# One-hot rows of the degree count: one tensor-with-tensor comparison per group of 512 ids in place of four per-column comparisons

## The reference, cut to what matters

```
ones    = jnp.ones((E,))
deg_in  = segment_sum(ones, dst, num_segments=N)
deg_out = segment_sum(ones, src, num_segments=N)
def layer(h, W, b, act):
    fwd = segment_sum(h[src], dst) / max(deg_in, 1)
    bwd = segment_sum(h[dst], src) / max(deg_out, 1)
    return act(concat([h, fwd, bwd]) @ W + b)
h = relu(layernorm(x));  x = x + layer(layer(h, W1, b1, relu), W2, b2, id)
h = relu(layernorm(x));  x = x + mlp(concat([h, segment_sum(edge_attr, dst), u[0]]))
```

## Time and profile before

| what | us |
|---|---|
| median of 3 executions | 4206.28 |
| fastest and slowest of them | 4197.02, 4271.05 |
| the profiled execution | 4203.99 |
| its span in the trace | 4202.4 |
| busy: PE, DVE, ACT, POOL | 3672.5, 3159.2, 2308.9, 3040.7 |
| first stage: first pick to last pick issued | 10.72 to 335.79 |

### The profile page before, as it was taken

The page is one execution under the profiler, slowest core; times in us unless marked ns, Lnnn a source line. Parts: engine busy times, 40 slices in busy tenths (PEclk is TensorE's granted clock), DMA queues, the critical chain, the costliest instruction groups (busy, mean ns, idle before and its releaser), DMA issues.

```text
span 4202.4 us, 94475 instructions
## 1 busy us (share of the span) xinstructions
PE 3672.5 (87%) x25698; PEld 3238.8 (77%) x25698; DVE 3159.2 (75%) x11005; ACT 2308.9 (55%) x5788; POOL 3040.7 (72%) x2962
## 2 busy tenths in 40 slices
PE   8817898888886888888888888699999999999999
PEld 2207888888876787887887787688888888888888
DVE  8816888888886555555565555489999999999998
ACT  0013444444444555555555555477777777777776
POOL 7866888888887677777777777666666666666665
PEclk9958999999998999999999999899999999999999
DMA  7676777777776677777787777777777777777775
GB/s 253 245 256 174 176 179 176 178 184 181 182 174 148 165 185 188 189 191 177 192 194 182 186 193 186 160 154 158 158 160 158 158 159 158 159 159 159 158 160 121
DMA packets 818427, 742.95 MB, mean 177 GB/s; under 512 B 200444, under 2 KB 629896, under 8 KB 818282
## 3 DMA queue, kind: packets, MB, share of 16 engines
q1 hardware_dynamic: 637702, 522.72, 42.0%
q0 software_dynamic: 166208, 167.10, 27.8%
q10 hardware_dynamic: 14372, 51.75, 3.1%
HBM read 355.07 MB, written 334.83 MB: 164 GB/s over the span
## 4 chain that ended last, share of the span: by engine, by line
PE 40%; DMA 7%; DVE 6%; issue 6%; another core or an unknown queue 4%; ACT 3%; SPq 2%; POOL 1%; DVEq 0%; ACTq 0%; POOLq 0%
PE bank L1569 8%; DMA normed<-in_x_dram 6%; PE bank L1583 4%; PE bank L1582 4%; PE bank L1584 4%; PE bank L1547 2%; PE bank L1540 2%; PE bank L1542 2%; PE bank L1546 2%; PE bank L1541 2%; PE bank L1556 2%; DVE stats L1169 2%; PE bank L1477 2%; PE bank L1478 1%
## 5 line engine op out<-in xcount | busy, mean ns | idle before, releaser
L632 POOL DMA_INDIRECT node<-summed,rep_index x392 | 624.7, 1594 | 230.6 <-issue 158.9
L585 POOL DMA_INDIRECT sums<-summed,rep_index x392 | 621.1, 1584 | 149.1 <-issue 122.2
L663 POOL TENSOR_TENSOR resid<-node_out,b3s 128x128 f32<-128x128 f32 x784 | 335.9, 457 | 478.4 <-DVE rows L1291 475.5
L1241 DVE SCALAR_TENSOR_TENSOR z<-bank,bias,small 128x512 f32<-128x512 f32 x784 | 568.0, 744 | 67.0 <-ACT small L897 58.3
L897 ACT ACTIVATE small<-bank,bias_small 128x512 f32<-128x512 f32 x784 | 535.4, 683 | 104.0 <-PE bank L1584 49.3
L673 POOL TENSOR_TENSOR z_lo<-z,z_hi 128x512 fp32r<-128x512 f32 x392 | 495.5, 1283 | 9.4 <-ACT z_hi L928 9.4
L1477 PE MATMUL bank<-hx,W1s 128*128 128x128 f32 x1568 | 325.2, 291 | 179.2 <-ACT hx L837 150.6
L617 POOL DMA_INDIRECT ends<-sums,index x392 | 381.6, 974 | 121.8 <-issue 121.5
L1477 PEld LDWEIGHTS bank<-hx,W1s 128*128 128x128 f32 x1568 | 251.1, 201 | 213.4 <-issue 213.2
L1569 PE MATMUL bank<-w3s,z 128*128 128x128 f32 x3136 | 382.4, 275 | 3.1 <-DVE z L1241 3.1
L1569 PEld LDWEIGHTS bank<-w3s,z 128*128 128x128 f32 x3136 | 365.7, 192 | 4.1 <-DVE z L1241 4.0
(11 more groups left out here) (152 smaller groups left out, 9549.8 us busy)
## 6 DMA issues: line engine op xcount, KB each, us to landing
node<-blank SPq DMA_DIRECT2D x98, 768.0 KB
sums<-zeros ACTq DMA_DIRECT2D x98, 512.0 KB
normed<-in_x_dram SPq DMA_DIRECT2D x196, 256.0 KB
rows<-sums SPq DMA_DIRECT2D x196, 256.0 KB
y<-node_out SPq DMA_DIRECT2D x196, 256.0 KB
node_out<-node SPq DMA_DIRECT2D x196, 256.0 KB, 3.2
node_out<-y POOLq DMA_DIRECT2D x196, 256.0 KB, 4.2
a_parts<-a_pair SPq DMA_DIRECT2D x784, 64.0 KB, 2.6
```

Of the source, the lines that this page charges most:

```text
L585: pool.indirect_dma_start(sums1, bass.IndirectOffsetOnAxis(ap=rep_index[:, b, s:s + 1], axis=0), summed[:, b, s, 0:F], None, compute_op=AL ...
L632: pool.indirect_dma_start(node1, bass.IndirectOffsetOnAxis(ap=rep_index[:, b, s:s + 1], axis=0), summed[:, b, s, :], None, compute_op=ALU. ...
L1241: dve.scalar_tensor_tensor(out=z[:, m, :], in0=bank[first_bank + m][:], scalar=bias[:, m:m + 1], in1=small[:, m, :], op0=ALU.add, op1=ALU. ...
```

## The change

Only the counting is touched. A group's four columns are compared in one instruction with each table: the tables `iota_hi` and `iota_lo` hold every value four times side by side, `hilo` is stored in f16 with the four columns of a group adjacent, and `tensor_tensor` compares the table with the four ids of the group, repeated along the table. The four one-hot rows of a group so lie interleaved: element (value, s) at position 4 * value + s. The buffers are two, each for a whole group. TensorE reads column s of the buffer with a step of four elements (8 bytes), for the stationary and for the moving operand. The counts and the banks are the same. The loop over groups is written out, as before.

```diff
-        iota_hi = sb("iota_hi", [P, HALF], F16)
-        iota_lo = sb("iota_lo", [P, 2 * P], F16)
+        iota_hi = sb("iota_hi", [P, HALF, 4], F16)
+        iota_lo = sb("iota_lo", [P, 2 * P, 4], F16)
...
-        hilo = sb("hilo", [P, 2, 4, G])
-        onehot_hi = sb("onehot_hi", [P, 4, HALF], BF16)
-        onehot_lo = sb("onehot_lo", [P, 4, 2 * P], BF16)
+        hilo = sb("hilo", [P, 2, G, 4], F16)
+        onehot_hi = sb("onehot_hi", [P, 2, HALF, 4], BF16)
+        onehot_lo = sb("onehot_lo", [P, 2, 2 * P, 4], BF16)
...
-            pool.iota(iota_hi[:], pattern=[[1, HALF]], base=0, channel_multiplier=0,
+            pool.iota(iota_hi[:], pattern=[[1, HALF], [0, 4]], base=0, channel_multiplier=0,
...
-            pool.iota(iota_lo[:], pattern=[[1, 2 * P]], base=0, channel_multiplier=0,
+            pool.iota(iota_lo[:], pattern=[[1, 2 * P], [0, 4]], base=0, channel_multiplier=0,
...
-            dve.tensor_copy(hilo[:].rearrange("p a s g -> p a (s g)"), part[:]).then_inc(s_vprep, 1)
+            for a in range(2):
+                last = dve.tensor_copy(hilo[:, a].rearrange("p g s -> p s g"), part[:, a].rearrange("p (s g) -> p s g", g=G))
+            last.then_inc(s_vprep, 1)
...
-            def onehots(st, i):
-                s = st.half + 2 * i
-                if st.after(2):
-
-                    dve.wait_ge(s_count, 2 * st.k + i - 3)
-                dve.tensor_scalar(onehot_lo[:, s, :], iota_lo[:], hilo[:, 1, s, bass.ds(st.g, 1)], None, ALU.is_equal)
-                dve.tensor_scalar(onehot_hi[:, s, :], iota_hi[:], hilo[:, 0, s, bass.ds(st.g, 1)], None, ALU.is_equal)\
+            for g in range(G):
+                b = g % 2
+                if g >= 2:
+
+                    dve.wait_ge(s_count, 4 * (g - 1))
+                dve.tensor_tensor(onehot_lo[:, b], iota_lo[:], hilo[:, 1, g, :].unsqueeze(1).to_broadcast([P, 2 * P, 4]), ALU.is_equal)
+                dve.tensor_tensor(onehot_hi[:, b], iota_hi[:], hilo[:, 0, g, :].unsqueeze(1).to_broadcast([P, HALF, 4]), ALU.is_equal)\
                     .then_inc(s_onehot, 1)
...
-            def count(st):
-                for i in range(2):
-                    s = st.half + 2 * i
-                    pe.wait_ge(s_onehot, 2 * st.k + i + 1)
+            for g in range(G):
+                pe.wait_ge(s_onehot, g + 1)
+                for s in range(4):
                     for h in range(2):
-                        last = pe.matmul(bank[2 * i + h][:, 0:HALF], onehot_lo[:, s, h * P:(h + 1) * P], onehot_hi[:, s, :],
-                                         start=(st.known and st.k == 0), stop=st.last)
+                        last = pe.matmul(bank[2 * (s // 2) + h][:, 0:HALF], onehot_lo[:, g % 2, h * P:(h + 1) * P, s],
+                                         onehot_hi[:, g % 2, :, s], start=(g == 0 and s % 2 == 0), stop=(g == G - 1 and s % 2 == 1))
                     last.then_inc(s_count, 1)
```

More of the change, by code:

```diff
@@ L277, in ticks @@
                 tick(lambda n, t=t: Step(STEPS // 4 - 1, t - n))
-        def written_out(tick):
-            for k in range(STEPS):
-                tick(lambda n, k=k: Step(0, k - n))
         QUADS = G // 4
@@ L981, in rstd_of @@
                 dve.reciprocal(rstd[:, st.b, 0:n], spread[:, st.b, 0:n]).then_inc(s_rstd, 1)
-            def onehots(st, i):
-                s = st.half + 2 * i
-                if st.after(2):
-                    dve.wait_ge(s_count, 2 * st.k + i - 3)
-                dve.tensor_scalar(onehot_lo[:, s, :], iota_lo[:], hilo[:, 1, s, bass.ds(st.g, 1)], None, ALU.is_equal)
-                dve.tensor_scalar(onehot_hi[:, s, :], iota_hi[:], hilo[:, 0, s, bass.ds(st.g, 1)], None, ALU.is_equal)\
-                    .then_inc(s_onehot, 1)
-            def tick(at):
-                st = at(0)
-                if st.exists:
-                    for i in range(2):
-                        onehots(st, i)
-            written_out(tick)
+            for g in range(G):
[4 more added lines that the diff above has]
+                dve.tensor_tensor(onehot_hi[:, b], iota_hi[:], hilo[:, 0, g, :].unsqueeze(1).to_broadcast([P, HALF, 4]), ALU.is_equal)\
+                    .then_inc(s_onehot, 1)
             def layer1():
```

## The result

The changed kernel takes 4331.06 us (median of 4, 4301.20 to 4340.79), before beside it 4238.66 (4 executions, 4197.02 to 4275.66): ratio 1.030, 95% interval 1.027 to 1.033. I had said 4187, the same within 2%. The profiled execution took 4328.36, its span is 4326.7, so the two spans differ by 124.3.

What follows compares the result with a forecast made beforehand. GpSimd's chain of picks, held up by VectorE's comparisons, was taken to bound the first stage. Picks 19 us earlier less 1 us for queued fills gave 18 us less than about 4204: 4187 us, range 4165 to 4216.

Steps and rivals of the forecast that it cites:

- What bounds the kernel: First stage: GpSimd's chain of 196 picks sets its end, slowed to 1.71 us a pick while VectorE compares, 1.25 after.
- the 44 us: Picks during the counting: 97 picks, each held up by 0.45 us, cost the chain some 44 us in all.
- The comparisons: VectorE in the counting: two tensor_tensor of 0.60 and 0.89 us, so 1.49 us a group against 1.72.
- the lower bound: Comparisons at the 2-byte tensor_scalar rate, 136 more elements costing 0.04 us: 1.0 us a group.
- The picks: GpSimd during the counting: picks held by tensor_tensor go in step with groups, 1.49 us each, lasting near 1.19.
- the 97th pick: First pick after the counting: forecast at 169.1 us against 188.32, 19 us earlier; the stage after it unchanged.
- The tables: The two iotas before the counting: 1176 + 768 more elements at 0.88 ns cost 1.7 us, on the path.
- TensorE: Counting matmuls: 0.176 us each, 1.41 a group, if the 8-byte step costs nothing, just under VectorE's 1.49.
- The rival of the slow TensorE: Counting: the step slows matmuls to 2.8 us a group, counting ends at 295, +30 us, 4234; chance 0.05.

Runs made afterwards that it cites:

- b2: The kernel before, unchanged, executed once more among the later executions: 4066.00 us.
- c1: Changed kernel with the four one-hot rows one behind the other, table repeated by an outer zero step, id by an inner one: 4219.11 us, ratio to before 1.033.
- p2: Changed kernel, but VectorE writes buffers nothing reads, TensorE reads only group 0's rows, and after group 0 neither waits for the other: 4145.29 us.
- e3: Changed kernel, but TensorE reads both operands packed, so other elements are counted: 4179.38 us, ratio to before 0.996.
- k2: Changed kernel with two columns interleaved in place of four, so TensorE's step is 4 bytes, same results: 4266.82 us, ratio to before 1.014.
- a1: The changed kernel, unchanged, executed again among the later executions: 4139.11 us, with before at 4084.24 beside it.
- b1: The kernel before, unchanged, executed once more among the later executions: 4074.86 us.
- e7: Changed kernel, but fixed rows are loaded by plain DMAs from ScalarE's queue instead of GpSimd's gathers: 4204.30 us.
- h1: Changed kernel, but high digits are compared by four tensor_scalar into packed rows, low digits stay interleaved, same results: 4194.15 us, ratio to before 0.999.
- e1: Changed kernel, but TensorE reads only its moving operand packed, so other elements are counted: 4186.36 us, ratio to before 0.996.
- e6: Kernel before with its tensor_scalar comparisons, but TensorE reads the moving operand with a step of four elements from rows four times as long: 4351.37 us.

## Why the prediction was wrong

- *What bounds the kernel* held: the picks set the end of the stage and their pace hangs on the comparisons. But the 1.71 was the rhythm of one execution; in `b2` before goes at 1.39, so the 44 us that the change was to win from were not there in every execution. The slack of the counting, 67 us in the profiled execution, I had read but not used as a limit: it says that the counting may grow by 67 and no more.
- *The comparisons* held: 0.60 and 0.89 forecast, 0.61 and 0.88 measured. The two elements a cycle that the Trainium skill gives on VectorE: DVE Perf Modes, section "The perf-mode tier table", are there, but only where the innermost step is not zero (`c1`). The 0.04 us for 136 elements in the lower bound is 0.05 by the starts of the rows (0.24 less 0.19); no other term uses it.
- *The picks* held for as long as VectorE is the bound: 1.49 and 1.19 forecast, 1.49 and 1.18 to 1.19 in `p2`. In `e3` the mean pace is 1.59, because TensorE's eight matmuls and the hand-over of two buffers need more than 1.49 in every second group; I had set TensorE's 1.41 aside as "just under". So in `e3` the 97th pick comes at 179.6 and not at 169.1, 9 us earlier than before and not 19. That the last one still comes at 317.9 for 317 is luck in part: the other 9 us come after the counting, where I had expected none. The hold of an indirect DMA that begins inside a `tensor_tensor` is real; the inference of the Trainium skill, SBUF — State Buffer, section "Who interferes with whom", that `tensor_tensor` does not stall a DMA, is not borne out for these indirect ones in `e3`, `p2` and `c1` (1.18, 1.19 and 2.53 instead of 0.95).
- *The tables* were mis-sized: 1.7 us forecast, 4.7 measured at TensorE's first instruction (11.78 against 7.06), and 4.4 at the first pick. `iota_hi` costs 2.94 us more, 2.5 ns for each of its 1176 more elements, not the 0.88 that two rows without repetition had given. Nor is it a price by element: in `k2` every value stands twice, 784 elements, and it takes 4.38. It is 3 us of 144.
- **The step that failed is *TensorE*.** I took 0.176 a matmul "if a step of 8 bytes costs nothing", by a row whose operands are packed, and gave the other bound 2.8 us a group and a chance of 0.05. Measured: 0.349, 2.79 a group, at the full clock as at the lower one (the guess of 2.8 came from the lower clock's row). The Trainium skill, SBUF — State Buffer, section "Specifications (TRN2)", asks for two hits in a line of 16 bytes for full bandwidth; a step of 8 bytes gives two, and here it runs at half. A step of 4 bytes runs at full rate (`k2`).
- *The rival of the slow TensorE* had the mechanism: counts complete at 295 (291.7 in `a1`), ScalarE waiting at the table (64 us). Its price, +30, can be worked out again: table at 293.8 plus 68.8 to the last pick is 362.6, +26.8 on before's 335.79, an estimate across two executions. Against the before of the later executions, which reaches its table earlier (52 us after its counts in `b1` and 23 in `b2`, not 67), less of the slow counting is hidden, and the loss measured is 55.
- *What no rival had* are the standstills, 92 us of the counting and, with the cover used up, as much of the end: 4204 + 26.8 + 92 = 4323, of the 4328 measured. This is an account and no test, as the 92 are what was left over in the same trace.

What the standstills are stays open. Shown: they need neither fills, nor `tensor_tensor`, nor slow matmuls. None was seen without GpSimd's picks beside the counting: `e7` has none (one execution), and no kernel has any after the picks pause. They appear among the earlier executions only, there in five profiled kernels out of nine heavily and in `h1` briefly, not in `e1`, `e3` and `e7`, nor in the comparisons of the profiled execution of before. The chip doesn't decide it: `h1`, `k2`, `e6`, `e7` ran on the one on which `a1` ran later. Whether VectorE or TensorE stops first wasn't told apart, since the kernels built for it were taken only among the later executions.

The traces of the two kinds differ in one more thing, and it is a rival that no run here settles. In every earlier trace 108 to 135 waits end at "remote", most of them in layers 1 and 2, and about a third of the semaphore updates is missing; in the later ones no wait ends so and none is missing to speak of (between 20 and 260 us 1418 updates in the profile of the changed kernel, 5557 in `a1`, and 5366 in `e7`, which has no standstill there). Updates also come late: before the comparison of 61.19 no update by TensorE is recorded between 44.9 and 60.4, though eight of its matmuls, from 50.84 to 53.80, lie in that time, and then six come between 61.12 and 61.34, 0.04 apart, where in `a1` they are 0.70 apart. So VectorE may well stand for an update that reaches it late. Whether the updates themselves are late or only their records, and whether the recording of an execution holds the engines up, is not known. If it does, the loss that belongs to the change is the 55 us of `a1` and not the 92.4 between the medians of the result (4331.06 and 4238.66). Before's own spread of 100 us among the earlier executions may be the same thing; this is only argued.

## What to carry to other kernels

A layout chosen for the engine that writes is read by another: before one-hot rows (or any operand) are interleaved, look at the step of the moving operand, for in bf16 8 bytes halved TensorE's rate and 4 bytes did not. Where a zero step is needed, put it outside: inside it halved VectorE's rate. And read the slack of a hidden piece of work as the limit to which it may grow: 67 us of cover were there, the change took 105 and more.

## What was not expected of the hardware

- A moving operand of 392 bf16 with a step of 8 bytes: 0.349 us a matmul at either level of the clock, against 0.17 to 0.18 packed or at 4 bytes at the full clock and 0.327 at the lower one. The same step in the stationary operand costs a weight load 117 ns instead of 99 and the pace nothing (`e1`).
- `iota` of f16 with its values repeated inside: 3.39 us for 392 values four times, 4.38 for 392 twice (`k2`), 0.45 for 392 once.
- With `tensor_scalar` picks and comparisons settle in more than one rhythm: a pick with four columns at 1.71 (before) or with three at 1.39 (`b2`), there with comparisons of 0.52 and 0.42 in place of 0.28 and 0.31. With `tensor_tensor` no run shows VectorE wait for a pick (`p2`: 1.49 throughout).
- VectorE and TensorE can stand for 5 to 18 us, by their rows with nothing left to do first, while GpSimd issues indirect DMAs; the trace lacks semaphore updates in these stretches.
